# Two-stage FFN with top-2 routing on one core: transposes of results next to transposes of inputs, VectorE's stage-two work in another order and in smaller parts

## The reference, cut to what matters

```python
# x: (32, 128, 128) float32: 4096 tokens of 128 values; itok: which of 16 small experts a sequence uses
h = gelu(x @ fc1_w.T + fc1_b)                                    # 128 -> 512
y = concat(h @ fc2_w.T + fc2_b, h @ experts_w[itok].T + experts_b[itok])   # 96 + 32 = 128
scores = y @ router_w.T                                          # 8 experts
top_v, top_i = top_k(scores, 2);  routing_w = softmax(top_v)
out = 0
for e in range(8):
    w_e = sum(where(top_i == e, routing_w, 0), axis=-1)
    out += (gelu(y @ expert_w1[e].T) @ expert_w2[e].T) * w_e[:, None]   # 128 -> 512 -> 128
return x + out
```

## Time and profile before

| | us |
|---|---|
| runs of the kernel before | 226.77, 227.58, 228.03 (median 227.58) |
| the profiled execution | 226.1, of which the span is 224.2 |
| PE busy | 204.3 (91% of the span), PE weight loads 174.4 |
| DVE busy | 166.0 (74%) |
| ACT busy | 143.1 (64%) |
| POOL busy | 150.0 (67%) |
| mean granted clock of TensorE | 0.978 of full speed |

### The profile page before, as it was taken

One profiled execution on the slowest core, in us unless ns is written; L12 is line 12 of the kernel. 1 busy time (PEld: TensorE's weight loads), 2 busy tenths in 40 slices (PEclk: granted clock), 3 DMA queues, 4 the chain that ended last, 5 costly groups with the idle time before them and its releaser, 6 DMA issues.

```text
span 224.2 us, 4074 instructions
## 1 busy us (share of the span) xinstructions
PE 204.3 (91%) x1259; PEld 174.4 (78%) x1259; DVE 166.0 (74%) x558; ACT 143.1 (64%) x259; POOL 150.0 (67%) x180
## 2 busy tenths in 40 slices
PE   7999999999899798989989999999999999999800
PEld 3999999999798576767868788786898788998600
DVE  1359999999878857598887889888766766737442
ACT  2778988875575387656666676676558777475410
POOL 5427777777777777777747565566777326777771
PEclk9999999999999979999999999999999999999995
DMA  5897884434272952997877765758699649998877
GB/s 171 255 312 239 307 266 132 138 98 137 78 291 78 386 222 77 367 384 303 264 305 270 260 236 188 262 187 282 228 317 404 235 168 294 372 404 293 263 244 292
DMA packets 25799, 56.11 MB, mean 250 GB/s; under 512 B 4872, under 2 KB 11280, under 8 KB 23218
## 3 DMA queue, kind: packets, MB, share of 16 engines
q1 hardware_dynamic: 20800, 47.27, 61.3%
q0 software_dynamic: 4544, 8.54, 11.0%
q10 hardware_dynamic: 434, 0.06, 0.2%
HBM read 22.76 MB, written 13.02 MB: 160 GB/s over the span
## 4 chain that ended last, share of the span: by engine, by line
PE 43%; POOL 26%; issue 10%; DVE 10%; DMA 7%; ACT 2%; SPq 1%; POOLq 0%; DVEq 0%
POOL slots L523 24%; PE hp L1037 14%; PE dd L1049 7%; PE misc L1049 7%; PE tr L1099 3%; PE hp L1072 3%; DMA results<-rows,back_row 3%; DVE hs L853 2%; PE dd L1020 2%; POOL results L531 2%; PE hp L971 2%; DMA z<-results 2%; PE hp L1012 1%; PE dd L1086 1%; PE dd L985 1%
## 5 line engine op out<-in xcount | busy, mean ns | idle before, releaser
L531 POOL DMA_INDIRECT results<-rows,back_row x78 | 78.5, 1007 | 41.4 <-DVE rows L866 20.8
L523 POOL DMA_INDIRECT slots<-y_rows,slot x64 | 65.5, 1023 | 25.8 <-issue 18.9
L1037 PE MATMUL hp<-xs,w 128*128 128x512 f32 x192 | 52.0, 407 | 3.2 <-DVE hs L853 3.2
L592 ACT ACTIVATE hp<-hp 128x1024 f32<-128x1024 f32 x34 | 34.3, 1010 | 28.7 <-PE hp L1037 28.7
L853 DVE TENSOR_TENSOR hs<-hp,hs 128x1024 fp32r<-128x1024 f32 x34 | 41.3, 1219 | 12.5 <-ACT hs L596 12.4
L1037 PEld LDWEIGHTS hp<-xs,w 128*128 128x128 f32 x192 | 35.6, 192 | 13.8 <-DVE hs L853 5.2
L596 ACT ACTIVATE hs<-hp 128x1024 fp32r<-128x1024 f32 x34 | 34.9, 1027 | 1.1
L985 PE MATMUL dd<-cond,hs_raw 128*128 128x128 f32 x256 | 35.4, 282 | 0.0
L985 PEld LDWEIGHTS dd<-cond,hs_raw 128*128 128x128 f32 x256 | 31.6, 192 | 0.2
L549 ACT ACTIVATE hs_raw<-hp,fc_bias 128x256 f32<-128x256 f32 x64 | 26.1, 468 | 4.6 <-PE hp L971 2.5
L968 PE MATMUL hp<-xs,w 128*128 128x256 f32 x168 | 26.2, 295 | 0.0
(11 more groups left out here) (156 smaller groups left out, 299.6 us busy)
## 6 DMA issues: line engine op xcount, KB each, us to landing
w<-ffn SPq DMA_DIRECT2D x20, 1024.0 KB, 5.4
picked<-slots SPq DMA_DIRECT2D x16, 264.0 KB, 4.4
ffn_raw<-in_wT SPq DMA_DIRECT2D x8, 512.0 KB, 5.1
z<-results SPq DMA_DIRECT2D x8, 512.0 KB, 4.3
cond<-in_cexpT SPq DMA_DIRECT2D x32, 80.0 KB
x_rows<-in_x SPq DMA_DIRECT2D x1, 2048.0 KB, 11.2
out<-z SPq DMA_DIRECT2D x8, 256.0 KB, 4.5
xs_raw<-in_xT SPq DMA_DIRECT2D x7, 256.0 KB, 3.6
```

The lines of the kernel that those rows point to most:

```text
L523: pool.indirect_dma_start(out=slots, out_offset=bass.IndirectOffsetOnAxis(ap=slot[:, p, n:n + 1], axis=0), in_=y_rows[:, p % YB, k, r, :], ...
L531: pool.indirect_dma_start(out=results, out_offset=bass.IndirectOffsetOnAxis(ap=back_row[:, t, r:r + 1], axis=0), in_=rows[:, t % RB, r, :] ...
L592: act.activation(gelu_of(t, g), up_of(t, g), ACT.Gelu).then_inc(c_gelu, 1)
L1037: mm = pe.matmul(hp[:, g, n * TILE:(n + 1) * TILE], w[:, t % WB, 0, part, f * P:(f + 1) * P], xs[:, (NP + t) % XB, v, :], start=m == 0, st ...
```

## The change

On **PE**, turn_out(t-2) moves from behind up(t, 1) to right behind up(t, 0), ahead of turn_in(t+1), in every pass (from pass 20 on it stood there already; the last three tiles' code is as it was). On **DVE**, in the passes of stage two, rows_of(t-2) moves ahead of low(t, 0) and picked_low(t+1). The **list work** is cut otherwise:

| pass | before | after |
|---|---|---|
| 2 | last_counts (15 instructions) | its first 5 |
| 3 | last_list | the other 10 (`last_wide`), and last_list |
| 4 | narrow_list | its first 6 (`narrow_origin`) |
| 5 | own_tiles | the rest of narrow_list |
| 6 | needed_tiles, chunks 0 and 1 | own_tiles |
| 7 to 9 | needed_tiles, two chunks each | needed_tiles, one chunk each |
| 10 | counted_signals | needed_tiles, one chunk |
| 11 to 14 | nothing | needed_tiles, one chunk each |
| 15 | nothing | awaited_tiles (2 instructions) |
| 16 | nothing | the rest of counted_signals (3 instructions) |

```diff
+            def last_wide():
                 link(dve.scalar_tensor_tensor(odd[:, :], full_of[:, :], -2.0, units[:, :], ALU.mult, ALU.add))
...
                 if wide(t - 1):
                     tile_low(t - 1, 1)
+                if t - 2 < FREE:
+                    rows_of(t - 2)
                 if wide(t):
                     tile_low(t, 0)
                 if t + 1 < BY_ACT:
                     picked_low(t + 1)
-                if t - 2 < FREE:
-                    rows_of(t - 2)
                 if not wide(t):
                     tile_low(t, 0)
+
                 if t == 2:
                     last_counts()
                 if t == 3:
+                    last_wide()
                     last_list()
                 if t == 4:
+                    narrow_origin()
+                if t == 5:
                     narrow_list()
-                if t == 5:
+                if t == 6:
                     own_tiles()
-                if 6 <= t <= 9:
-                    needed_tiles(2 * (t - 6), 2 * (t - 5))
-                if t == 10:
+                if 7 <= t < 7 + CHUNKS:
+                    needed_tiles(t - 7, t - 6)
+                if t == 7 + CHUNKS:
+                    awaited_tiles()
+                if t == 8 + CHUNKS:
                     counted_signals()
...
                     narrow_up(t)
-                if t >= BY_ACT:
-                    turn_out(t - 2)
+                turn_out(t - 2)
                 if t + 1 < TILES:
                     turn_in(t + 1)
...
                 if wide(t):
                     tile_up(t, 1)
-                if t < BY_ACT:
-                    turn_out(t - 2)
                 if wide(t - 1):
                     tile_down(t - 1, 1)
```

More of the change, by code:

```diff
@@ L786, in last_list, with narrow_origin @@
                 dve.sem_inc(s_list, 1)
-            def narrow_list():
+            def narrow_origin():
                 link(dve.scalar_tensor_tensor(odd[:, :], taken[2][:, :], -2.0, units[:, :], ALU.mult, ALU.add))
@@ L794, in narrow_list @@
                 link(dve.scalar_tensor_tensor(origin[:, :], left[:, :], float(TILE), origin[:, :], ALU.mult, ALU.add))
+            def narrow_list():
                 list_tiles(FIRST_NARROW, LATE_WIDE, (LATE_NARROW, TILES), upto[:, :], 1)
@@ L804, in own_tiles, with awaited_tiles @@
                                        after[:, :].unsqueeze(2).to_broadcast((P, TILES, EXP)), ALU.mult))
-            def counted_signals():
+            def awaited_tiles():
                 link(dve.tensor_scalar(need_f[:, :], need_f[:, :], float(RB), None, ALU.max))
@@ L810, in counted_signals @@
                                        after[:, :].unsqueeze(1).to_broadcast((P, CHUNKS, TILES)), ALU.is_ge))
+            def counted_signals():
                 dve.wait_ge(s_shares, SHARES)
```

## The result

The changed kernel took 229.24 us in the median of 20 runs (226.53 to 230.92, and one of 703.8), the kernel before, on the same chip, 227.82 (225.93 to 230.06, 20 runs). The ratio is 1.0068, with a 95% interval of 1.0039 to 1.0097; all ratios here leave out the runs that lie more than 1.5% above the fastest of their kernel. So it is slower, by about 1.5 us (1.4 by the medians), where 2.2 were forecast. The profiled execution took 229.02 us, with a span of 227.1 (before 226.1 and 224.2).

The account below looks back on a forecast made before the run. Tile 19's scatter was taken to bound the kernel, through PE's delivery and POOL's queue. Scatter 0.6 later plus one clock fall of 1.6 gave 2.2 on 227.58: 229.8 us, range 227.3 to 231.8.

Parts of the forecast that it names:

- The waits: PE's turn_out waits for DVE's copy: 2.4 us in pass 4, 0.3 in 6, 1.4 in 13, 2.8 in 14.
- The turns side by side: Joining the two transpose groups on PE gains nothing; at most 0.1 us a pass, 1.8 in all.
- The start: PE starts pass 3 0.35 us earlier, as tile 0's turn falls into the wait for picked rows.
- PE in all: PE delivers tile 19 3.0 us later, or 2.2 to 3.8, before any fall of the clock.
- The waits that go: PE's waits for DVE's differences, 3.6 us between passes 3 and 12, disappear.
- POOL: The 2.6 us scatter queue nearly vanishes; tile 19's scatter starts 0.4 to 0.9 us later, 0.6 taken, without a fall.
- The clock: Long stretches in passes 4 and 14 endanger PE's clock; one of two brings a fall, costing 1.6 us.
- The end: The span grows from 224.2 to 226.4 us, 2.2 later, with tile 19's scatter and the last chunk setting it.
- Without a fall: Rival: PE's clock doesn't fall in pass 4 or 14; 228.2 us, chance 0.25.
- both falling: Rival: PE's clock falls in both pass 4 and pass 14; 231.4 us, chance 0.18.
- the crowded end: Rival: x and chunk loads start 2 us later and collide with tiles 17 to 19; about 230.5 us, chance 0.10.
- Faster: Rival: DVE is in time in the narrow passes, so 4.2 us of waits don't come; 225.0 us, chance 0.12.

Follow-up runs that it names:

- the fourth chip: The changed kernel itself run again on another chip, against the kernel before there: ratio 0.986, median 267.71 us.
- e1_lists: Against the changed kernel: new list parts kept, PE and DVE back in the orders of before; ratio to before 1.006 on the second chip, 0.994 on the fourth.
- e2_orders: Against the changed kernel: new PE and DVE orders kept, list work in its old portions; ratio to before 0.983 on the second chip, 0.984 on the fourth.
- e4_late1314: The changed kernel with turn_out and rows_of back in their old places in passes 13 and 14; ratio to before 0.983, on a third chip 0.985.
- e3_fill: The changed kernel plus eight bf16 matmuls of 512 columns ahead of turn_out in passes 4 and 14; ratio to before 0.980, on a third chip 0.986.

## Why the prediction was right, point by point

- **The waits: right, each at its place.** 2.4, 0.3, 1.4 and 2.8 were worked out for passes 4, 6, 13 and 14; PE lost 2.57, 0.36, 1.44 and 2.76 (2.42, 0.21, 1.28 and 2.58 in the brackets of the rows). On the fourth chip, with its stops, the brackets of passes 4, 13 and 14 have 2.57, 2.31 and 1.04, so the last two sizes hold for the first chip only. The method was to follow DVE's work from the start of the pass, instruction by instruction, against the moment at which PE asks. Where it is off, by 0.17 in pass 4, the list part was longer than summed: its first instruction starts at 101.22 and flat at 105.50, 4.28 against 4.02. (The rows: DVE after, pass 3.)

```profile
101.22 0.16 DVE L776 SCALAR_TENSOR_TENSOR odd<-full_of,units 128x8 f32<-128x8 f32 x1
...
105.50 0.69 DVE L865 COPY yT<-dd 128x512 f32<-128x512 f32 x1
```

- **The turns side by side: mis-sized.** This term was taken as 0, with 0.1 a pass as the end of the range, and measured 0.12. The rows explain it. Before, each pass had two groups of down-projection, and each stood behind a turn and took 146.96 - 145.48 = 1.48:

```profile
145.48 1.64 PE L1049 MATMUL misc<-hs,w 128*128 128x512 f32 x6
146.96 1.55 PE L1037 MATMUL hp<-xs,w 128*128 128x512 f32 x6
```

After, the one behind the turns takes 147.03 - 145.58 = 1.45, the one behind other matmuls 149.75 - 148.40 = 1.35; the two turns together take 145.58 - 144.79 = 0.79 instead of 0.71; the ups save 0.02 each. Sum: -0.13 - 0.03 + 0.08 - 0.04 = -0.12. The failed step was to look for a gap in the rows and find none. The sign stood in the earlier trace rows, had I split the pass: up, behind matmuls, took 1.39, and the same number of matmuls of the same size behind a turn 1.48.
- **The start: wrong.** Pass 3 was to begin 0.35 earlier; it began 0.18 later (95.75 against 95.57), since the picked rows of the turn before it landed later, at 91.16 against 90.51.
- **PE in all: right by two errors.** 3.0 and a fall of 1.6 were forecast for tile 19, 4.6 in all, and 4.44 measured. The shorter passes gave about 1.1 up to tile 12. Against this stand the 0.5 at the start and what the waits cost above the forecast.
- **The waits that go: right.** No wait of up for hs is left up to tile 12.
- **POOL: right.** The queue was to be as good as gone, with tile 19 from 0.4 to 0.9 later without a fall. Tile 19's scatter starts at 211.31; the forecast with a fall was 209.14 + 0.6 + 1.6 = 211.34.
- **The clock: right in size; the number is in part luck.** 1.6 were forecast for a fall, and 1.57 and 1.35 measured. One fall of two came, in pass 14, but the trace has one execution, and the same kernel's on the fourth chip has two. By the rule of the Trainium skill ("TensorE: Matmul & The Clock Gate", section "Why this matters for your kernels") both stretches were in danger; of the stops counted above, 18 of 21 had a fall, which agrees.
- **The end: a little short.** 2.85 in the span of the profiled execution against 2.2: the last chunk's load took 1.31 longer and the scatter's landing 0.63 less. In the medians it is 1.4. A likely reason, not shown, is that not every execution has the fall that the profiled one has: the mean granted clock of the runs, the one of 703.8 aside, goes from 0.964 to 0.982, with 0.971 in the profiled one. The trace shows only one of them.
- **The rivals.** Without a fall (228.2), both falling (231.4) and the crowded end (230.5) are within 2 us of the result, and single executions may have been any of them. Faster (225.0) didn't happen here, though it did on the fourth chip, by none of the reasons that I gave: as far as the traces tell, the changed kernel avoids a stop that the profiles of the first chip don't contain.

## What to carry to other kernels

A wait is priced by following the engine that delivers, instruction by instruction, to the moment at which the other asks; done so, four waits came out within 0.2 us, and filler work belongs where its engine is idle, ahead of the instruction it would wait at, not in front of the one that others wait for. When groups of matmuls are reordered, split the pass into its groups and compare the same group behind different neighbours, even when no gap shows. And a gain or loss of 1% can have another sign on another chip: compare stage by stage from landmarks in the trace before explaining a ratio.

## What the runs showed that I had not expected

- Six matmuls of 512 columns take 1.48 us (before) or 1.45 (after) behind a group of transposes and 1.35 to 1.39 behind other matmuls.
- Three other chips took 271 to 273 us for the kernel that takes 227.8 on the first, some 35 of it ahead of the turn-in of tile 3. In stage two e1_lists stops at the same instructions on two chips, up to 5 us at a time (in e2_orders not every stop repeats), and another order of PE's and DVE's instructions moves the stops of ACT, whose own instructions are unchanged.
- Eight matmuls of 512 columns in bf16, put into a wait of 2.57 us, cost nothing: the wait shrank to 0.83, and the pass was as long as in e4_late1314 (9.14 and 9.13).
- Tiles of padding, whose rows are dropped, can still set the end: in e4_late1314 and e3_fill the last scatter ended 2.71 us behind the last addition.
